# A two-layer gated convolution on one core: first weights transposed by VectorE, last image in four shorter blocks

## The reference, cut to what matters

```python
def qconv_cg(x, w, theta):
    yp = conv3x3(x[:, :16], w[:, :16])
    yr = conv3x3(x[:, 16:], w[:, 16:])
    d = sigmoid(2.0 * (yp - theta))
    return yp + d * yr

h = relu(bn(qconv_cg(x, w_a, theta_a), gamma_a, beta_a, mean_a, var_a))
h = bn(qconv_cg(h, w_b, theta_b), gamma_b, beta_b, mean_b, var_b)
return relu(x + h)
```

## Time and profile before

| | |
|---|---|
| median of 3 runs | 434.52 us (434.52 to 435.0) |
| profiled execution | 434.99 us |
| its span, first to last instruction | 433.1 us |
| TensorE busy | 426.2 us (98%) |
| VectorE busy | 246.1 us (57%) |
| ScalarE busy | 198.7 us (46%) |
| GpSimd busy | 30.8 us (7%) |
| first real product | 6.48 us |
| mean granted TensorE clock | 0.996 |

### The profile page before, as it was taken

How to read it: one execution, slowest core, us unless ns; L and a number is a source line. 1 busy time by engine, 2 the same in 40 slices (tenths; PEclk the granted TensorE clock), 3 DMA queues, 4 the chain that set the end, 5 groups by cost and what they waited for, 6 DMA issues and landing times.

```text
span 433.1 us, 17330 instructions
## 1 busy us (share of the span) xinstructions
PE 426.2 (98%) x7823; PEld 423.9 (98%) x7823; DVE 246.1 (57%) x423; ACT 198.7 (46%) x338; POOL 30.8 (7%) x81
## 2 busy tenths in 40 slices
PE   9999999999999999999999999999999999999994
PEld 8999999999999999999999999999999999999993
DVE  6767644753764663574375385366357367436535
ACT  5765444534544553453453453354345355434322
POOL 6041000000000100000000000021000000000001
PEclk9999999999999999999999999999999999999998
DMA  8435116251615110420624161161623321012044
GB/s 166 87 79 98 27 27 123 50 98 29 122 28 101 25 28 4 99 51 2 125 57 82 37 123 29 27 123 25 122 49 62 66 49 39 13 27 49 8 93 94
DMA packets 119802, 27.57 MB, mean 64 GB/s; under 512 B 119408, under 2 KB 119664, under 8 KB 119728
## 3 DMA queue, kind: packets, MB, share of 16 engines
q1 hardware_dynamic: 117760, 26.09, 29.7%
q10 hardware_dynamic: 1648, 0.36, 0.4%
q0 software_dynamic: 320, 0.00, 0.0%
HBM read 13.60 MB, written 12.85 MB: 61 GB/s over the span
## 4 chain that ended last, share of the span: by engine, by line
PE 98%; DVE 1%; issue 0%; ACT 0%; DVEq 0%
PE acc L549 96%; PE acc L500 1%; DVE mix L863 0%; DVE rows_out L911 0%; PE acc L575 0%; PE acc L488 0%; ACT mix L697 0%; PE acc L492 0%; DVE rows_out L953 0%; DVE rows_out L908 0%; ACT rows_out L719 0%; DVEq L862 0%
## 5 line engine op out<-in xcount | busy, mean ns | idle before, releaser
L549 PE MATMUL acc<-x_lo,w_hi 32*128 32x456 f32 (+1 forms) x1392 | 251.3, 358 | 0.0
L549 PE MATMUL acc<-x_hi,w_lo 32*128 32x456 f32 (+1 forms) x1392 | 250.8, 358 | 0.0
L549 PE MATMUL acc<-x_hi,w_hi 32*128 32x456 f32 (+1 forms) x1392 | 250.5, 357 | 0.0
L549 PE MATMUL acc<-h_hi,w_lo 32*128 32x512 f32 x1152 | 244.2, 390 | 0.0
L549 PE MATMUL acc<-h_lo,w_hi 32*128 32x512 f32 x1152 | 243.7, 389 | 0.0
L549 PE MATMUL acc<-h_hi,w_hi 32*128 32x512 f32 x1152 | 243.5, 389 | 0.0
L549 PEld LDWEIGHTS acc<-x_lo,w_hi 32*128 32x128 f32 x1392 | 212.0, 183 | 0.0
L549 PEld LDWEIGHTS acc<-x_hi,w_lo 32*128 32x128 f32 x1392 | 211.8, 183 | 0.1
L549 PEld LDWEIGHTS acc<-x_hi,w_hi 32*128 32x128 f32 x1392 | 211.7, 183 | 0.0
L549 PEld LDWEIGHTS acc<-h_hi,w_hi 32*128 32x128 f32 x1152 | 183.9, 183 | 0.1
L549 PEld LDWEIGHTS acc<-h_hi,w_lo 32*128 32x128 f32 x1152 | 183.4, 183 | 0.0
(11 more groups left out here) (86 smaller groups left out, 161.3 us busy)
## 6 DMA issues: line engine op xcount, KB each, us to landing
out_dram<-rows_out SPq DMA_DIRECT2D x95, 126.0 KB, 2.5
x<-in_x_dram SPq DMA_DIRECT2D x28, 392.0 KB, 5.3
early<-in_x_dram SPq DMA_DIRECT2D x4, 112.0 KB, 3.7
x<-in_x_dram SPq DMA_DIRECT2D x4, 98.0 KB, 3.2
out_dram<-rows_out SPq DMA_DIRECT2D x3, 112.0 KB, 2.4
x<-in_x_dram SPq DMA_DIRECT2D x1, 294.0 KB, 4.3
x<-in_x_dram SPq DMA_DIRECT2D x1, 280.0 KB, 5.0
x<-in_x_dram SPq DMA_DIRECT2D x1, 196.0 KB, 3.5
```

Source lines behind the costliest of these rows:

```text
L549: return pe.matmul(sums(bank, blk), w[g * ROWS:(g + 1) * ROWS, tap], moving(blk, part, c, dx, g), start=(u == 0 and (alone or g == bank_gr ...
```

## The change

It has three parts. The first weights are loaded like the second ones, by group, in four DMAs (two by SP, two by ScalarE), and transposed by VectorE; TensorE's transposes and all that served them go, the zeros grow from 9 to 10 products and the bridge from 1 to 3. ScalarE, not VectorE, makes the first block's high part of x, and x's third part has a load of its own. The short blocks of layer a remain for one pair of images instead of two. The last image's second convolution is cut in four blocks of 7, 7, 7 and 6 slots instead of three of 9 (with the edge rows in "e", as before).

```diff
-SHORT, SHORT_PAIRS = 7, 2
+SHORT, SHORT_PAIRS = 7, 1
+LAST = (7, 7, 7, 6)
-WARM, BRIDGE = 9, 1
-WARM_BANK, TAP_BANK = 3, 4
+WARM, BRIDGE = 10, 3
+WARM_BANK = 4
...
-        second += [("b", 3 * img + r) for r in range(3)]
+        second += [("b", 3 * img + r) for r in range(3 if img < B - 1 else len(LAST))]
...
-    second[-4:] = [second[-3], second[-2], second[-4], second[-1], ("e", 1)]
+    second[-5:] = second[-4:-2] + [second[-5], second[-2], second[-1], ("e", 1)]
     def b_slots(n):
+        r = n - 3 * (B - 1)
+        if r >= 0:
+            return B - 1, 1 + sum(LAST[:r]), LAST[r]
         return n // 3, 1 + n % 3 * BLK_B, BLK_B
...
+        natural = sb("natural", [P, 5, HALF_NAT])
+        w_t = sb("w_t", [P, 2 * TAPS, P])
...
+        def load_w(eng, w, g, done):
+            eng.dma_start(natural[g * ROWS:(g + 1) * ROWS, 1:4:2],
+                          w.rearrange("(h o) (g i) a b -> g o h (i a b)", h=2, g=GROUPS)[g]).then_inc(done, 16)
...
-            sp.dma_start(w_nat_a, w_a.rearrange("o i a b -> o (i a b)")).then_inc(w_landed[0], 16)
+            for g in (0, 1):
+                load_w(sp, w_a, g, w_landed[0])
             sp.wait_ge(xpads_zero, 1)
             load_x(sp, 0, 0, SHORT + 1, x_first[0], (0,))
             load_x(sp, 0, SHORT + 1, 2 * SHORT + 1, x_second)
-            load_x(sp, 0, 2 * SHORT + 1, XS, x_landed[0])
+            load_x(sp, 0, 2 * SHORT + 1, 3 * SHORT + 1, x_third, (0,))
+            load_x(sp, 0, 3 * SHORT + 1, XS, x_landed[0])
...
+            sp.wait_ge(wt_ready[0], 2)
             for g in range(GROUPS):
+                load_w(sp, w_b, g, w_landed[1])
...
             for n in range(WARM):
                 zeros_product(BANK)
-            pe.wait_ge(ident_ready, 2)
-            for c in range(2):
-                weights(c, 6 + c)
             for n in range(BRIDGE):
                 zeros_product(P)
...
                 if step == 24:
+                    pe.wait_ge(ident_ready, 2)
...
                             pe.wait_ge(xhi0_ready, 1)
-                            pe.wait_ge(wtap_ready, 1)
+                            pe.wait_ge(whi_ready, 1)
...
-                    if u == 0 and b == TAP_BANK and g == bank_groups(b)[0]:
-                        pe.wait_ge(wlo_ready, 1)
-                    if g == 0 and u == 0 and b == 1:
-                        pe.wait_ge(wlo_ready, 2)
...
+            for g in (2, 3):
+                load_w(nc.scalar, w_a, g, w_landed[0])
             act.wait_ge(xpads_zero, 1)
             load_x(nc.scalar, 0, 0, SHORT + 1, x_first[0], (1,))
-            weights_odd()
-            weights_hi(0, TAP_BANK, 0, 1).then_inc(wtap_ready, 1)
-            weights_hi(0, 6, 1, TAPS).then_inc(whi_ready, 1)
-            weights_hi(1, 7, 0, TAPS).then_inc(whi_ready, 1)
+            act.wait_ge(probe_zero, 1)
+            nc.scalar.activation(probe[:, 2:3], probe[:, 2:3], ACT.Copy)
+            load_x(nc.scalar, 0, 2 * SHORT + 1, 3 * SHORT + 1, x_third, (1,))
+            act.wait_ge(wt_ready[0], 1)
+            weights_hi(0, slice(0, TAPS)).then_inc(whi_ready, 1)
             act.wait_ge(xcols_zero, 1)
+            act.wait_ge(x_first[0], 32)
+            nc.scalar.activation(split_chunk(x_hi, 0), x_chunk(0), ACT.Copy).then_inc(xhi0_ready, 1)
+            act.wait_ge(wt_ready[0], 2)
+            weights_hi(0, slice(TAPS, 2 * TAPS)).then_inc(whi_ready, 1)
             for n in range(1, SOON):
                 split_hi(n)
...
+            def transposed(k, c):
+                for mq in range(2):
+                    for h in range(2):
+                        rows = filter_rows(natural[:, 2 * h:2 * h + 3].rearrange("p z n -> p (z n)"),
+                                           2 * c - mq + 1, slice(0, TAPS))
+                        to = w_t[:, c * TAPS:(c + 1) * TAPS].rearrange("p t (o q) -> p t o q", q=2)
+                        last = nc.vector.transpose(to[:, :, h * ROWS:(h + 1) * ROWS, mq],
+                                                   rows.rearrange("p i q b -> p b i q"))
+                last.then_inc(wt_ready[k], 1)
+            def first_weights():
+                dve.wait_ge(w_landed[0], 16 * GROUPS)
+                dve.wait_ge(wzeros_ready, 1)
+                for c in range(2):
+                    transposed(0, c)
+                for c in range(2):
+                    dve.wait_ge(whi_ready, c + 1)
+                    weights_lo(0, c)
...
-            dve.wait_ge(x_first[0], 32)
-            nc.vector.tensor_copy(split_chunk(x_hi, 0), x_chunk(0)).then_inc(xhi0_ready, 1)
-            dve.wait_ge(wtap_ready, 1)
-            weights_lo(0, TAP_BANK, 0, 1)
-            dve.wait_ge(whi_ready, 1)
-            weights_lo(0, 6, 1, TAPS).then_inc(wlo_ready, 1)
-            dve.wait_ge(whi_ready, 2)
-            weights_lo(1, 7, 0, TAPS).then_inc(wlo_ready, 1)
+            first_weights()
```

More of the change, by code:

```diff
@@ L127, in slots_of @@
         kind, n = blk
-        return BLK_B if kind == "b" else EDGE if kind == "e" else sum(k for img, t, k in a_slots[n])
+        return b_slots(n)[2] if kind == "b" else EDGE if kind == "e" else sum(k for img, t, k in a_slots[n])
     def leading(blk):
@@ L248, in gated_conv_pair_kernel @@
         x_second = sem("x_second")
+        x_third = sem("x_third")
         x_landed = [sem(f"x_landed{n}") for n in range(X_IMGS)]
@@ L480, in _ @@
         def _(pe):
[L481 to L487, removed]
-                        last = pe.transpose(to[:, mq], w_pad[:, 2 * c - mq + 1, dx].rearrange("o i q -> o (i q)"),
-                                            ident[:])
-                    last.then_inc(wt_ready, 1)
-                    pe.matmul(psum[:, WARM_BANK, 0:C * 2], zeros(P)[C:P], zeros(P)[C:P], start=True, stop=True)
             def zeros(n):
@@ L758, in _ @@
             zero_x_pads(0, 1)
+            nc.vector.memset(natural[:, 0:5:2], 0.0).then_inc(wzeros_ready, 1)
             zero_x_pads(1, X_IMGS)
@@ L764, in _ @@
             nc.vector.memset(probe[:], 0.0).then_inc(probe_zero, 1)
-            for q in range(2):
-                nc.vector.memset(w_pad[:, TAPS * q, :, :, q], 0.0).then_inc(wpad_ready, 1)
-            nc.vector.memset(zeros_b, 0.0).then_inc(wzeros_ready, 1)
-            dve.wait_ge(w_landed[0], 16)
-            for dx in range(TAPS):
-                nc.vector.tensor_copy(w_pad[:, 1, dx], natural_a(slice(0, 2))[:, :, dx].rearrange("o a i -> o i a")
-                                      ).then_inc(wpad_ready, 1)
@@ new lines, in weights_lo @@
+            def weights_lo(k, c):
+                taps = slice(c * TAPS, (c + 1) * TAPS)
+                nc.vector.tensor_tensor(w_lo[k][:, taps], w_t[:, taps], w_hi[k][:, taps].bitcast(F32),
+                                        ALU.subtract).then_inc(wlo_ready, 1)
+            def first_weights():
[6 more added lines that the diff above has]
+                    weights_lo(0, c)
@@ L781, in second_weights @@
             def second_weights():
                 dve.wait_ge(w_landed[1], 16 * GROUPS)
-                dve.wait_ge(wzeros_ready, 1)
                 for c in range(2):
-                    for mq in range(2):
-                        for h in range(2):
-                            at = AT_B + 2 * h * HALF_NAT
-                            rows = filter_rows(early[:, at:at + 3 * HALF_NAT], 2 * c - mq + 1, slice(0, TAPS))
-                            to = w_t[:, c * TAPS:(c + 1) * TAPS].rearrange("p t (o q) -> p t o q", q=2)
-                            last = nc.vector.transpose(to[:, :, h * ROWS:(h + 1) * ROWS, mq],
-                                                       rows.rearrange("p i q b -> p b i q"))
-                    last.then_inc(wbt_ready, 2)
+                    transposed(1, c)
@@ L795, in second_weights_lo @@
             def second_weights_lo(c):
                 dve.wait_ge(whi_ready, 3 + c)
-                taps = slice(c * TAPS, (c + 1) * TAPS)
-                nc.vector.tensor_tensor(w_lo[1][:, taps], w_t[:, taps], w_hi[1][:, taps].bitcast(F32),
-                                        ALU.subtract).then_inc(wlo_ready, 1)
+                weights_lo(1, c)
             chain = [0]
```

59 lines of the change are left out of this document (12 added, 47 removed).

## The result

The changed kernel takes 436.37 us (median of 7 runs, 435.96 to 437.3), the kernel before, run beside it, 434.81 (7 runs, 434.52 to 435.22): ratio 1.0035, 95% interval 1.0024 to 1.0046. So it is slower by 1.56 us, outside the range that I gave (433.4 to 436.3). Its profiled execution (437.30 us, span 435.5) is its slowest; differences between single profiles are to be read with that in mind.

What follows compares the result with a forecast made beforehand. TensorE's unbroken line of products was taken as the bound, with head and tail around it. 434.99 - 0.4 (head) + 0.7 (tail and pace) = 435.3 us, 434.8 in terms of the runs' median; range 433.4 to 436.3.

Steps and rivals of the forecast that it cites:

- All at nothing: Head: later x loads, second weights and identity matrix are covered by other work and cost 0 us.
- I take +1.4: Pace of the products: a row group's lead beyond about 0.5 us is lost; last product +1.1 to +1.8 us.
- The gain at blocks 8 to 11: Pace there: 456 beside 512 columns gives a lead of 0.45, nothing lost, 0.4 us gained back.
- 0 (leads free): Lower bound of the pace term: row groups may run ahead of one another at no cost, 0 us.
- I carry -0.4: Head: first real product at 6.0 instead of 6.48 us, range -0.8 to +0.5, carried as -0.4 us.
- the clock at nothing: Head: TensorE's gap of 0.4 us before the first real products does not lower the clock, 0 us.
- tail: After the last product: shorter last blocks and stores; stores give -0.5 us, tail and pace together +0.7.
- B: Rival, pace: leads free or small blocks cheap, pace +0.06, in all -1.1 us, 433.4; chance 0.17.
- C: Rival, head: clock rises late after TensorE's silence from 5.6 to 6.0, +2.1 us, 436.9; chance 0.10.
- D: Rival, head: first weights' loads land at 4.9 instead of 3.9 us, +1.0, 435.8; chance 0.10.
- E: Rival, pace: no lead at all, each step lasts its longest product, +4.0 instead of +1.4, 437.4; chance 0.03.
- F: Rival, head: TensorE starts no earlier since x or second half of weights is late, 435.2; 0.60 together with forecast.

Runs made afterwards that it cites:

- early refills: Changed kernel with SyncE issuing the refill of x's ring ahead of the image's last store instead of behind it: 435.88 us, ratio 1.0015.
- the blocks alone: Kernel before with only the new blocks (one short pair, last image 7, 7, 7, 6) and their order, old head: 436.52 us, ratio 1.0039.
- the head alone: Changed kernel's new head with the old blocks (two short pairs, last image in three blocks of 9): 434.73 us, ratio 0.9998.
- the full version: Changed kernel with refills ahead of the store, second weights' transposes behind block 2 and the last eight blocks reordered: 434.42 us, ratio 0.9987.
- the orders: Changed kernel with its last blocks reordered: 435.51 us (6, 9, 7 slots last), 436.52 (order forecast as worse), 435.39 (best order, transposes also behind block 2).
- with eight: Eight instead of ten products of zeros: 434.75 us with the new head and old blocks, 434.62 in the 434.42 us version.

## Why the prediction was wrong, point by point

The forecast was 434.8, the result 436.37, 1.6 more. Three steps of the prediction failed.

1. *"All at nothing"*, the list of what hides the rest. I followed the queues at the head, and never the queue of refills, though the change moves most blocks of layer a by a place. Measured: the loss falls by 0.49 with a run that changes nothing but the refills' place. It stands in no term and no rival of the prediction; it is the one new mechanism. It could have been seen in the code and the trace of before: the split of image 13 at 302.22 and the refill's landing at 290.6 (5.36 after 285.25) leave less than the 16 us that a round takes.
2. *"I take +1.4"* for the lead. The mechanism was right and shown by order alone; its size was too small. With early refills the stretch from visit 8 to the last product is 393.55 against 391.81: +1.74, the columns' 0.06 among it. I had +1.1 to +1.8 and took the middle of the windows 12 to 16, where 12 would have given the size. The last two rounds lost 0.54 and 1.23 against the columns' pace, 1.77 where I had 1.25. The gain at blocks 8 to 11 was there, 0.27 to 0.37 against 0.4 in the changed kernel and with the blocks alone (0.06 to 0.43 over all profiles with the new blocks). My lower bound, "0 (leads free)", was a mistake of its own: worked out without a window, the code's waits for a bank alone cost some +1.2 to +1.5 from visit 8 to the last product.
3. *"I carry -0.4"* for the head. The weights did land earlier, and group 3's first visit ends 0.63 earlier in the changed kernel's profile; 0.25 earlier with the head alone. At the end that is -0.08 (head alone), -0.15 (changed against blocks only) and -0.42 (in the full version). I had TensorE's zeros end at 5.6, although ten of them at 0.46 us and three of a quarter of the columns come to 5.8; they ended at 5.85 to 5.92 in most profiles. With fewer of them the clock is at risk. I put the clock at nothing, and it wasn't. Group 1, which has no lead to spend, comes out of its first visit at 9.77 to 9.87 in profiles where the clock rose at 6.5 us or later, and at 9.37 to 9.58 where it rose by 6.1 (one exception, 9.73), with the old head at 9.86 to 10.26. So a late rise costs some 0.3 us of the head's gain. Between -0.1 and -0.4, this term's size stays open: its differences are as large as the spread of 0.3 between medians.

With what was measured the sum is -0.2 (head) + 1.74 (pace) + 0.49 (refills) - 0.5 (tail) = +1.5, against 1.56. The close agreement is partly luck: the head and the refills are differences of medians, the pace and the tail differences of single profiles, and from one profile to the next such a stretch varies by some tenths.

**What was right.** The tail: last product 429.88, gating directly behind it, the last sum behind GpSimd's addition, and stores landing in 2.3 to 2.7 us instead of 2.5 to 3.3, together -0.5. Less was lost at blocks 8 to 11. But the last product, forecast at 428.0, came at 429.88.

**The rivals.** B (leads are free, pace +0.06) is refuted by the orders, which move the time by 0.86 us at equal columns. C did not come with ten zeros beyond the 0.3 us of point 3, and did with eight, in some runs. D did not come: the last of the four loads landed at 3.2 to 3.7 in all profiles. E: the Trainium skill, "TensorE: Matmul & The Clock Gate", Part 3, "What overlaps and what doesn't", has products start and end strictly in program order. No trace here agrees: beside visits of 4.19 us others take 2.80 and 3.27, and a reordering of equal blocks moves the end by 1.4 us; the +4.0 that it would mean was far off. F is not borne out as I wrote it: real products did start 0.5 us earlier, and what took the gain back was none of its causes (point 3).

## What to carry to other kernels

When row groups of TensorE share one program order, equal work per group isn't enough: in this kernel a group could run ahead of the others by about a dozen products of the order (some 0.5 us), and a lead beyond it was lost inside "busy". Put blocks of different size so that each group's lead is worked off before the next, and go through the order product by product ahead of choosing it. And when blocks move by one place, check every engine that works by rounds: a place across a round's boundary moves its loads' due time by a whole round.

## What the runs showed of the hardware

- The rise of TensorE's granted clock came between 3.8 and 6.8 us after the start in the 14 profiles in which TensorE was not silent ahead of it, with nearly the same work. In the changed kernel's profile it rose at 3.8, and a silence of 0.8 us behind that (4.94 to 5.70) did not lower it: its steps from 6.0 on take 0.18 us. In the two profiles with eleven warming products it came at 10.3 behind a silence of 0.8 us, and at 9.2 behind one of 0.5; most other runs of these two kernels (16 of 23) were as quick as with ten zeros.
- The column of the granted clock says 1.00 up to the first record of a rise, even where products take 0.33 us a step; in the first microseconds only the durations tell.
- Four loads of 36 KB as the first transfers landed 1.7 to 2.5 us after their issue in two queues, the same form in the midst of x traffic took 2.4 to 3.7; x behind them landed later, image 1's at 12.7 to 14.4 instead of 11.9 to 12.1.
